# One-hots of a lot made by four VectorE instructions instead of one, its products by eight instead of four

## What is computed

```python
Wh = (h @ W.T + b).reshape(N, HEADS, HEAD_DIM)              # N=6250, 4 heads of 64
alpha_src = einsum('nhd,hd->nh', Wh, a_src)
alpha_dst = einsum('nhd,hd->nh', Wh, a_dst)
e   = leaky_relu(alpha_src[idx_i] + alpha_dst[idx_j], 0.2)  # one row per edge
ex  = exp(e - segment_max(e, idx_i)[idx_i])
att = ex / segment_sum(ex, idx_i)[idx_i]
out = segment_sum(att[:, :, None] * Wh[idx_j], idx_i)       # idx_i=src, idx_j=dst
```

## Time and profile before

| | us |
|---|---|
| median of 3 runs (lowest, highest) | 3393.16 (3389.64, 3396.11) |
| profiled execution, its own time | 3393.59 |
| its span in the trace | 3391.8 |
| VectorE busy | 1906.6 (56%) |
| TensorE matmuls busy | 2288.1 (67%) |
| GpSimd busy | 2156.6 (64%) |
| ScalarE busy | 773.7 (23%) |

### The profile page before, as it was taken

The page is one execution under the profiler, slowest core; times in us unless marked ns, Lnnn a source line. Parts: engine busy times, 40 slices in busy tenths (PEclk is TensorE's granted clock), DMA queues, the critical chain, the costliest instruction groups (busy, mean ns, idle before and its releaser), DMA issues.

```text
span 3391.8 us, 41019 instructions
## 1 busy us (share of the span) xinstructions
PE 2288.1 (67%) x10919; PEld 1564.2 (46%) x10920; DVE 1906.6 (56%) x3902; ACT 773.7 (23%) x1397; POOL 2156.6 (64%) x2140
## 2 busy tenths in 40 slices
PE   0000466664477787877878787877877878787877
PEld 0000233332355555555555555555555555555555
DVE  5999321212455656556665656556664565646564
ACT  0000122221132222222222222222222222222222
POOL 0002777401676777777777777777777777777771
PEclk9555677877698988888899998989897988998888
DMA  2200011102333343444434443443434444343453
GB/s 64 108 0 1 26 44 32 38 28 52 103 94 106 100 122 101 109 115 102 122 102 123 103 122 102 109 117 102 123 101 106 120 102 122 102 122 102 111 108 38
DMA packets 271469, 305.58 MB, mean 90 GB/s; under 512 B 164198, under 2 KB 210796, under 8 KB 271020
## 3 DMA queue, kind: packets, MB, share of 16 engines
q0 software_dynamic: 97760, 251.60, 27.9%
q1 hardware_dynamic: 140038, 18.08, 3.4%
q10 hardware_dynamic: 33480, 33.36, 3.0%
HBM read 276.25 MB, written 26.62 MB: 89 GB/s over the span
## 4 chain that ended last, share of the span: by engine, by line
PE 39%; POOL 15%; DVE 11%; issue 9%; ACT 2%; DMA 1%; DVEq 0%; POOLq 0%; SPq 0%; ACTq 0%
PE sum_banks L937 20%; POOL gathered L863 15%; PE f_banks L952 8%; DVE onehot L1340 3%; PE turned L909 2%; PE f_banks L996 1%; DVE gathered L1361 1%; PE f_banks L1071 1%; DMA gathered<-table,col 1%; PE sum_banks L925 1%; PE f_banks L977 1%; PE f_banks L1072 1%; PE f_banks L978 1%; PE f_banks L966 1%; DVE he L1489 1%
## 5 line engine op out<-in xcount | busy, mean ns | idle before, releaser
L863 POOL DMA_INDIRECT gathered<-table,col x1872 | 1898.5, 1014 | 595.1 <-issue 564.5
L937 PE MATMUL sum_banks<-gathered,onehot 128*128 128x260 f32 x3744 | 1061.8, 446 | 104.9 <-DVE gathered L1361 104.0
L937 PEld LDWEIGHTS sum_banks<-gathered,onehot 128*128 128x128 f32 x3744 | 818.4, 224 | 294.9 <-issue 132.5
L1361 DVE TENSOR_TENSOR gathered<-gathered 128x512 f32<-128x512 f32 x936 | 591.4, 692 | 47.2 <-ACT gathered L1116 44.4
L1340 DVE TENSOR_TENSOR onehot<-iota_row,col 128x1024 f32<-128x1024 f32 x236 | 289.0, 1225 | 472.7 <-PE sum_banks L937 442.9
L270 POOL DMA_INDIRECT edge_list<-payload,pos x244 | 248.0, 1016 | 377.9 <-DVE pos L387 300.6
L1112 ACT COPY onehot_t<-turned 128x1024 bf16<-128x1024 bf16 x236 | 238.7, 1011 | 392.0 <-PE turned L909 391.4
L1126 ACT COPY acc<-sum_banks x234 | 88.0, 376 | 877.3 <-PE sum_banks L937 726.5
L909 PE MATMUL turned<-ident_bf,onehot 128*128 128x128 bf16 x1888 | 158.5, 232 | 190.2 <-DVE onehot L1340 189.8
L582 PE MATMUL bank<-ident,y 128*128 128x128 f32 x104 | 25.6, 427 | 278.0 <-DVE y L469 278.0
L909 PEld LDWEIGHTS turned<-ident_bf,onehot 128*128 128x128 bf16 x1888 | 116.1, 103 | 208.4 <-DVE onehot L1340 169.7
(11 more groups left out here) (304 smaller groups left out, 2722.6 us busy)
## 6 DMA issues: line engine op xcount, KB each, us to landing
gathered<-table,col POOLq DMA_INDIRECT x1872
table<-wh ACTq DMA_DIRECT2D x13, 520.0 KB, 3.1
xn<-y ACTq DMA_DIRECT2D x13, 512.0 KB, 2.9
xn_batch<-xn ACTq DMA_DIRECT2D x13, 512.0 KB, 4.0
x_all<-in_x SPq DMA_DIRECT2D x1, 6144.0 KB
x_batch<-in_x ACTq DMA_DIRECT2D x12, 512.0 KB
out<-xf ACTq DMA_DIRECT2D x12, 512.0 KB
edge_list<-xn_all SPq DMA_DIRECT2D x2, 2176.0 KB, 13.8
```

The source lines that it names most:

```text
L863: g.indirect_dma_start(gathered[:, l, t, :], None, sh["table"], bass.IndirectOffsetOnAxis(ap=col[l][:, t // G, t % G, 0:1], axis=0)).then_ ...
L937: last = t.matmul(sum_banks[:, ds(banks_of[g], 1), 0:TB].rearrange("p a w -> p (a w)"), onehot[:, l % 3, g * G + k, :], gathered[:, l, g * ...
L1361: v.tensor_tensor(value, value, gathered[:, l, tiles, C:TB].unsqueeze(3).broadcast_to([P, G, H, HD]), ALU.mult).then_inc(s_mul, 1)
```

## The change

The one-hot matrix of a lot (8 tiles, 1024 columns) is made by four instructions of 2 tiles each, and the signal `s_sel` comes with the last. `product` takes one tile instead of two, so a lot has eight of them, and each signals `s_mul`. TensorE still waits for both tiles of a group, by counts of tiles. Nothing else differs. Lines behind L1340 stand 3 to 5 lines later.

```diff
@@ sums (TensorE)
                 for g in range(GROUPS):
-                    pe.wait_ge(s_mul, n * GROUPS + (g + 1))
+                    pe.wait_ge(s_mul, n * TILES + (g + 1) * G)
@@ select (VectorE)
-                v.tensor_tensor(onehot[:, l % 3, :, :], iota_row[:, :].unsqueeze(1).broadcast_to([P, TILES, P]),
-                                within.broadcast_to([P, TILES, P]), ALU.is_equal).then_inc(s_sel[l], 1)
+                for g in range(GROUPS):
+                    tiles = slice(g * G, g * G + G)
+                    last = v.tensor_tensor(onehot[:, l % 3, tiles, :],
+                                           iota_row[:, :].unsqueeze(1).broadcast_to([P, G, P]),
+                                           within[:, tiles, :].broadcast_to([P, G, P]), ALU.is_equal)
+                last.then_inc(s_sel[l], 1)
@@ product (VectorE)
-            def product(it, l, g):
-
-                tiles = slice(g * G, g * G + G)
-                value = gathered[:, l, tiles, 0:C].rearrange("p k (a d) -> p k a d", d=HD)
-                v.tensor_tensor(value, value, gathered[:, l, tiles, C:TB].unsqueeze(3).broadcast_to([P, G, H, HD]),
+            def product(it, l, tile):
+
+                value = gathered[:, l, tile, 0:C].rearrange("p (a d) -> p a d", d=HD)
+                v.tensor_tensor(value, value, gathered[:, l, tile, C:TB].unsqueeze(2).broadcast_to([P, H, HD]),
                                 ALU.mult).then_inc(s_mul, 1)
@@ lot (VectorE)
-                for g in range(GROUPS):
-                    product(it, l, g)
+                for tile in range(TILES):
+                    product(it, l, tile)
```

## The result

| | us |
|---|---|
| before, median of 6 runs (lowest, highest) | 3392.95 (3389.64, 3400.24) |
| changed, median of 6 runs (lowest, highest) | 3446.93 (3431.49, 3456.59) |
| ratio, 95% interval | 1.0152 (1.0125 to 1.0178) |
| profiled execution of the changed kernel, own time (span) | 3449.68 (3447.5) |

The changed kernel is 1.5% slower. The forecast was 3368 us and its range ended at 3394.

A forecast was written before the change was run, and what follows sets the result against it. GpSimd's queue of gathers was taken as the bound from 1120 us on. The terms, -34 + 9 + 0 = -25 us against the profiled 3393.6, gave 3368 us, with an 8-in-10 range of 3344 to 3394.

The forecast's parts named there:

- Term 1, the gathers: GpSimd's gathers L863: shorter VectorE instructions hold them less, excess falls from 122 to 88 us, gain 34 us (4 to 67).
- Term 2, the start: Lots 0 to 23, up to 1120 us, where GpSimd waits for the sums: slower lots lose 9 us (0 to 13).
- Term 3, the backlog: After 1120 us: slower lots cost nothing while the other engines catch up with GpSimd in each batch; 0 us (0 to 18).
- a cover of 138 us: VectorE's waiting for fetched rows plus TensorE time the clock gives back, set against 95 us of slower lots and GpSimd's lead.
- such waits over 20 us: Sign of being wrong: GpSimd's waits after 1120 us grow past 20 us, meaning the backlog reached it.
- The first part of the cover: VectorE's 79.8 us of waiting for fetched rows, in 33 lots, taken as room for slower lots.
- The second part: TensorE's sums regain the higher clock when VectorE waits less: at most 116 us over 33 lots, half of it assumed.
- The last lot: At the end rows land late and VectorE waits 5.59 us for them, so a longer backlog is hidden there.
- The slower rival: Sums, one-hots, products in mix and feed-forward lots: VectorE's added time becomes the bound, +44 us, 3438 us; chance 0.07.
- short trains catch nearly always: Rival at the gathers: short trains catch nearly every one, excess 118 us, 3398 us (halfway 3384); chance 0.12.
- the old pattern: Rival at the gathers: they pass trains unhurt as before, factor 0.50, excess 55 us, 3335 us; chance 0.10.
- the lock is per instruction: A VectorE instruction with two SBUF inputs holds a gather until its own end; rival that it isn't so: 3403 to 3423, chance 0.04.

The follow-up runs named there:

- a pause: Kernel before plus a VectorE memset of 128 columns that nobody reads, ahead of each one-hot instruction: 3436.96 us, ratio 1.0131; the same memset behind the products: 1.0000.
- trimming: Against the kernel with one-hots by four alone (1.0128): each one-hot instruction writes 104 of 128 columns, so the train keeps about its old length: 3372.73 us, 0.9943.
- both parts trimmed: Changed kernel with one-hots cut to 104 of 128 columns and products to 56 of 64 words of a head: 3375.38 us, ratio 0.9949.

## Why the prediction was wrong

- **Term 1, the gathers: right in size, not in its working.** Gain 34 us forecast, 37 measured, mean 994 ns against 996. Trains of 1.43 and 2.77 us were forecast at 1.455 and 2.835. The one-hots gave the gain (41.7 us; alone they brought the mean to 987 ns). The products took 15.1 us, and alone they raised the mean to 1033. The two errors cancel in part, which is luck. The median fell by 3 ns.
- **Term 2, the start: right.** 9 us (0 to 13) forecast; GpSimd's waits up to 1120 us rose from 26.9 to 34.4 us.
- **Term 3, the backlog, is the step that failed.** It had the addition right (0.23 us a lot for the one-hots, 0.21 measured; the products off the path in plain lots), and put against it a cover of 138 us, so that the term was 0. The runs showed 72.7 us more of GpSimd's waits after 1120 us (3.7 to 76.4) and 21.4 us more behind the last gather. The text had named such waits over 20 us as the sign of being wrong.
  - The first part of the cover, VectorE's 79.8 us of waiting for fetched rows, was there and was used up: it shrank by 63 us, to 17.2. But it lay in 33 lots, and the addition comes in all 234.
  - The second part, 58 us by "that comes back", the clock, wasn't there. The trace of before could have told: the sums of those 33 lots take 4.72 us on average and those of the other lots 4.51, so some 7 us could come back. The lot of 2559.41 isn't typical; 15 of the 33 had slow sums. With the waits gone the sums took 1064.3 us in all, where they had taken 1061.8.
  - Even without that part the prediction's own bound for the term was 18 us (95 - 80 is 15). The rest is the price of the ring, which was put at its length. It measured more: 49 us where a pause adds 19, and 63 us where trimming takes 47 away. The granted clock fell from 0.837 to 0.826, the opposite of what was counted on. Why the ring costs more than its length, and how much of that is the clock, stays open.
- **The last lot.** "A longer backlog is hidden there" was wrong too. The last eight gathers stand behind a wait of 7.36 us. The last of them starts at 3359.8, and VectorE comes to its rows 25 us later, without waiting for them, where before it came 15 us later after a wait of 5.59 us. At the end it is the backlog that is worked off, and nothing hides it:

```profile
3350.66 0.94 POOL L863 DMA_INDIRECT gathered<-table,col  x1 [7.36 <-PE sum_banks L937]
...
3385.17 0.35 DVE L1353 TENSOR_REDUCE scored<-scores 128x64 f32<-128x192 f32 x1
```

- **The slower rival was the right one in kind.** "VectorE's added time becomes the bound", with 3438 us, had the outcome, and was given 0.07. It put the place in the products of the mix and feed-forward lots and the point of decision at 0.34 us a lot. The one-hots' 0.21 us and, without any split, a pause of 0.08 us were enough. Its sum counted a lot's loss once, at its length.
- **The other rivals.** Gathers that short trains catch nearly always (1012 ns by its excess), and the old pattern (978 ns), are both refused by 994 ns. That the lock is per instruction agrees with the trimmed kernels: the same trains, cut into four, gave 53 us of gathers. It has exceptions. The longest gather of the changed kernel, forecast near 2 us, took 3.58: it starts at 1284.49, with a train of eight products that ends at 1287.25, and 2.76 + 0.82 = 3.58, so it was held to the train's end. Three of the 619 gathers held in short trains were held for more than one instruction; with both parts trimmed it was 14, for up to 1.74 us. The Trainium skill, page "SBUF — State Buffer", section "Who interferes with whom", reports that tensor_tensor was not seen to stall DMA and gives a reason that it calls inferred. These traces show the opposite for gathers whose indices lie in SBUF.
- **VectorE's busy time** was forecast to rise by 247 us and rose by 104.6. Instructions in a train overlap, and the page counts the overlap once: 49.7 us more for the one-hots and 56.5 for the products, about 234 x (0.2 + 0.24).

## What to carry to other kernels

The queue that bounds the kernel shows what a faster one would give, but not how much the others can lose. For that, find the ring with the least room (here sums, one-hots, transposes, sums) and test it before the change by a cheap pause in it and the same pause beside it: 0.08 us in the ring cost 1.3%, and behind the products nothing. Ask of waiting time that is to be cover in which lots it lies. And before counting on a clock that gives something back, compare in the trace of before the lots that wait with those that don't (here 4.72 and 4.51 us).

## What the runs showed of the hardware that was not expected

- How sharply VectorE holds a gather. In the kernel before, a gather that starts 0.03 us behind a one-hot instruction takes its usual 0.95 us, and one that starts 0.05 us behind it is held until that instruction has ended, and then needs 0.82 us more (1297.04 + 1.23 + 0.82 = 1299.09; it ends at 1299.08):

```profile
1858.89 1.29 DVE L1340 TENSOR_TENSOR onehot<-iota_row,col 128x1024 f32<-128x1024 f32 x1 [3.96 <-PE sum_banks L937]
1858.92 0.95 POOL L863 DMA_INDIRECT gathered<-table,col  x1 [0.30 <-PE sum_banks L937]
...
1297.04 1.23 DVE L1340 TENSOR_TENSOR onehot<-iota_row,col 128x1024 f32<-128x1024 f32 x1 [0.63 <-PE sum_banks L937]
1297.09 1.99 POOL L863 DMA_INDIRECT gathered<-table,col  x1 [0.30 <-issue]
```

- The gathers' mean length depends on how lots and gathers fall together, not only on the instructions in their way: 1014 ns before, 1030 with the bank numbers loaded early and not one VectorE instruction changed, 1033 with products of half the length. The same one-hot instruction held the gathers for 66.9, 110.0 and 98.2 us in these three.
- A delay of 0.08 us in each of 234 lots, 19 us in all, costs 49 us of 3388. The granted clock of TensorE falls from 0.837 to 0.824 with it, and in the two trimmed kernels, which are faster, it is 0.841 and 0.840. But it is 0.822 with the bank numbers loaded early, where GpSimd waits for no more than before. How much of the price is the clock, and how much comes from the meeting of the engines in the mix and feed-forward lots, stays open.
- Between transposes and the clearing matmul stood 0.28 or 0.90 us without a wait, and 1.22 us in a lot in which the transposes had started early; nothing is seen there when the bank numbers are loaded ahead of the transposes. So a register load on TensorE's queue was part of the path.
- A memset of 0.17 us ahead of a dependent train delays it by 0.08 us only: the one-hot instruction starts at 1745.82, 0.09 us before the memset of 1745.74 has ended.
